# Gate logits of a cross-attention and mixture-of-experts block: gate weights held still in four column groups, tokens streamed

## The reference

```python
x = x + xattn(layernorm(x), ctx, ctx, mask, wq, bq, wk, bk, wv, bv, wo, bo)
xn2 = layernorm(x).reshape(8192, 512)
scores = softmax(xn2 @ w_gate)                 # [8192, 8]: the gate
weights, idx = top_k(scores, 2)
# each expert takes its tokens (at most 2048): h = xe @ c_fc; a, g = split(h)
# y = (silu(a) * g) @ c_proj; the sum of both, times their weights, is added to x
```

## Time and profile before

| | |
|---|---|
| median of 3 runs | 3031.32 us (3030.25 to 3031.86) |
| profiled execution | 3035.1 us, its span 3033.3 us |
| mean granted TensorE clock | 0.984 |
| busy, share of the span | TensorE 97%, weight loads 82%, VectorE 51%, ACT 51%, POOL 42% |

### The profile page before, as it was taken

How to read it: one execution, slowest core, us unless ns; L and a number is a source line. 1 busy time by engine, 2 the same in 40 slices (tenths; PEclk the granted TensorE clock), 3 DMA queues, 4 the chain that set the end, 5 groups by cost and what they waited for, 6 DMA issues and landing times.

```text
span 3033.3 us, 55379 instructions
## 1 busy us (share of the span) xinstructions
PE 2938.5 (97%) x17824; PEld 2489.2 (82%) x17824; DVE 1533.9 (51%) x5034; ACT 1542.7 (51%) x3910; POOL 1262.6 (42%) x1911
## 2 busy tenths in 40 slices
PE   6999999999999999994999999999999999999998
PEld 6888888888888888883788888888888888888886
DVE  5777777777777777773433223333242332423331
ACT  4777777777777777772323223233232322322321
POOL 4566666666666666664112122222212121222211
PEclk8999999999999999996999999999999999999999
DMA  5444444444444444432534343344434443444322
GB/s 162 124 126 132 124 122 127 126 132 124 124 126 125 133 125 124 125 104 83 135 87 101 77 98 78 90 88 91 86 94 88 94 94 77 98 80 94 68 44 28
DMA packets 290390, 315.35 MB, mean 104 GB/s; under 512 B 46528, under 2 KB 234944, under 8 KB 288576
## 3 DMA queue, kind: packets, MB, share of 16 engines
q1 hardware_dynamic: 227040, 178.48, 22.5%
q0 software_dynamic: 32768, 67.26, 12.8%
q10 hardware_dynamic: 30304, 66.07, 6.7%
HBM read 109.53 MB, written 67.90 MB: 58 GB/s over the span
## 4 chain that ended last, share of the span: by engine, by line
PE 51%; DMA 1%; SPq 0%; issue 0%; POOL 0%; DVE 0%; ACT 0%; POOLq 0%
PE a_ps L1219 17%; PE g_ps L1219 17%; PE y_ps L1234 17%; DMA out<-y,recs 0%; SPq L1012 0%; DMA xg<-xn_rows,gather_ids 0%; POOL xg L1058 0%; DMA lists<-table 0%; DMA x_quarters<-xg 0%; DVE xe_lo L1153 0%; POOL out L1086 0%; ACT xe_hi L1113 0%; DVE x_turned L1166 0%; ACT y L1146 0%; DVE act_part L1166 0%
## 5 line engine op out<-in xcount | busy, mean ns | idle before, releaser
L1086 POOL DMA_INDIRECT out<-y,recs x128 | 207.2, 1618 | 1185.7 <-ACT y L1146 751.8
L373 POOL TENSOR_SCALAR probs<-probs,row_inv 128x256 f32<-128x256 f32 x1024 | 492.3, 493 | 417.0 <-DVE row_inv L586 412.6
L577 DVE CUSTOM_DVE_ANT_0 probs<-scores_ps,mask_add,row_any 128x256 f32<-128x256 f32 x1024 | 454.6, 480 | 272.2 <-PE scores_ps L793 269.3
L1193 DVE TENSOR_TENSOR hidden<-act_part,g_ps 128x512 f32<-128x512 f32 x192 | 132.1, 688 | 860.0 <-ACT act_part L1132 860.0
L477 ACT ACTIVATE probs<-probs,low 128x256 f32<-128x256 f32 x1024 | 513.7, 504 | 99.9 <-DVE low L577 85.9
L462 ACT COPY probs_t<-probs_t_ps 128x512 f32<-128x512 f32 x512 | 299.9, 586 | 193.9 <-PE probs_t_ps L805 145.0
L1219 PE MATMUL a_ps<-xe_hi,fc_hi 128*128 128x512 f32 x768 | 300.3, 391 | 39.7 <-DVE xe_lo L1153 39.4
L805 PE MATMUL probs_t_ps<-ident,probs 128*128 128x128 f32 x2048 | 310.8, 274 | 7.5 <-POOL probs L373 7.5
L1219 PE MATMUL a_ps<-xe_lo,fc_hi 128*128 128x512 f32 x768 | 299.6, 390 | 0.0
L1219 PE MATMUL a_ps<-xe_hi,fc_lo 128*128 128x512 f32 x768 | 299.5, 390 | 0.0
L1219 PE MATMUL g_ps<-xe_lo,fc_hi 128*128 128x512 f32 x768 | 298.8, 389 | 0.0
(11 more groups left out here) (170 smaller groups left out, 6656.1 us busy)
## 6 DMA issues: line engine op xcount, KB each, us to landing
k_stack<-qk_hi SPq DMA_DIRECT2D x512, 64.0 KB, 2.0
q_stack<-qk_hi SPq DMA_DIRECT2D x512, 64.0 KB, 2.8
x_quarters<-xg SPq DMA_DIRECT2D x512, 64.0 KB, 2.0
fc_raw<-in_c_fc SPq DMA_DIRECT2D x24, 1024.0 KB, 5.8
k_stack<-qk_lo SPq DMA_DIRECT2D x256, 64.0 KB, 2.0
q_stack<-qk_lo SPq DMA_DIRECT2D x256, 64.0 KB, 2.9
out<-x_xn ACTq DMA_DIRECT2D x32, 512.0 KB, 3.3
xn_rows<-x_xn ACTq DMA_DIRECT2D x32, 512.0 KB, 3.6
```

The lines of the kernel that those rows point to most:

```text
L373: last = nc.gpsimd.tensor_scalar(probs[:, r, t, :], probs[:, r, t, :], row_inv[:, r, t:t + 1], 1.0, ALU.mult, ALU.mult)
L577: last = nc.vector.tensor_tensor_reduce(out=probs[:, s % 4, t, :], in0=scores_ps[s % 2][:, t, :], in1=mask_add[:, t, :], scale=row_any[:, ...
L1086: nc.gpsimd.indirect_dma_start(out=out[:, :], out_offset=bass.IndirectOffsetOnAxis(ap=recs[:, i * CT + t, 0:1].bitcast(U32), axis=0), in_= ...
L1193: nc.vector.tensor_tensor(hidden[:, m % 2, :], act_part[:, m % 2, :], g_ps[m % 2][:, :], ALU.mult).then_inc(gated, 1)
```

## The change

The gate weights are put into groups of 32 columns (`wg` is [128, 4, 32], cleared first, with the eight real columns loaded into each group). For each chunk c one matmul takes `wg[:, c, :]` as the stationary operand and all 256 tokens of the chunk as the moving one, and writes the partitions 32c to 32c+31 of `bank_b`: four partial products, transposed (experts in partitions), side by side. ACT copies them to `gate_parts` in SBUF. Two more matmuls, one for each tile of tokens, take `gate_parts` as the stationary operand and the constant `sum_parts` (a one where the partition is 32c + e for expert e) as the moving one; they add up the four parts and give the logits in the layout of before.

In the slots: the two transposes are at slots 10 and 11 and both go into `bank_a`, at slot 11 ahead of the matmuls of L820, so the second waits for the copy of the first. The gate matmuls are at slot 12 and wait for both copies; ACT's copy of the parts is at slot 12, the summing matmuls at slot 13. On POOL one more clearing stands first in the block, and a clearing with four selections behind its other constants. SP's load of wg waits for the clearing.

```diff
--- before.py
+++ after.py
@@ -98,7 +98,9 @@
         w_hi = sb("w_hi", [P, 4, DC, D], F32R)
         w_lo = sb("w_lo", [P, 4, DC, D], F32R)
         w_parts = (w_hi, w_lo)
-        wg = sb("wg", [P, DC, EXPERTS])
+
+        wg = sb("wg", [P, DC, DK])
+        sum_parts = sb("sum_parts", [P, EXPERTS])
         bias_qk = sb("bias_qk", [P, 2, DC])
         bias_v = sb("bias_v", [P, DC])
         bias_o = sb("bias_o", [P, D])
@@ -146,6 +148,7 @@
         shifted = sb("shifted", [P, 2, TILES])
         rstd = sb("rstd", [P, 2, TILES])
 
+        gate_parts = sb("gate_parts", [P, SEQ])
         logits = sb("logits", [P, TILES, EXPERTS])
         top = sb("top", [P, TILES, 8])
         top_at = sb("top_at", [P, TILES, 8], U32)
@@ -220,6 +223,10 @@
         xn2_stored = sem("xn2_stored")
         x2t_full = sem("x2t_full")
         x2t_ready = sem("x2t_ready")
+        wg_cleared = sem("wg_cleared")
+        sum_parts_ready = sem("sum_parts_ready")
+        gate_full = sem("gate_full")
+        gate_copied = sem("gate_copied")
         logits_full = sem("logits_full")
         logits_copied = sem("logits_copied")
         route_step = sem("route_step")
@@ -288,7 +295,8 @@
                         load_x(sp, 0, 0)
                         load_c(sp, 0)
                         load_w(0)
-                        sp.dma_start(wg[:, :, :], w_gate).then_inc(setup_loaded, 16)
+                        sp.wait_ge(wg_cleared, 1)
+                        sp.dma_start(wg[:, :, 0:EXPERTS], w_gate).then_inc(setup_loaded, 16)
                         sp.dma_start(bias_qk[:, :, :], b_qk).then_inc(setup_loaded, 16)
                         sp.dma_start(bias_v[:, :], b_v).then_inc(setup_loaded, 16)
                         sp.dma_start(bias_o[:, :], b_o).then_inc(setup_loaded, 16)
@@ -316,6 +324,7 @@
 
             @block.gpsimd
             def _(pool):
+                nc.gpsimd.memset(wg[:, :, :], 0.0).then_inc(wg_cleared, 1)
                 nc.gpsimd.memset(ident[:, :], 0.0).then_inc(pool_const, 1)
                 nc.gpsimd.memset(before[:, :], 0.0).then_inc(pool_const, 1)
                 nc.gpsimd.memset(zeros, 0.0).then_inc(pool_const, 1)
@@ -337,6 +346,13 @@
                                channel_multiplier=0, allow_small_or_imprecise_dtypes=True).then_inc(pool_const, 1)
                 nc.gpsimd.iota(tok_ids[:, :], pattern=[[P, TILES]], base=0, channel_multiplier=1,
                                allow_small_or_imprecise_dtypes=True).then_inc(pool_const, 1)
+
+                nc.gpsimd.memset(sum_parts[:, :], 0.0).then_inc(sum_parts_ready, 1)
+                for c in range(DC):
+                    pool.wait_ge(sum_parts_ready, c + 1)
+                    nc.gpsimd.affine_select(out=sum_parts[:, :], in_=sum_parts[:, :], compare_op=ALU.not_equal,
+                                            fill=1.0, base=-c * DK, pattern=[[-1, EXPERTS]],
+                                            channel_multiplier=1).then_inc(sum_parts_ready, 1)
 
                 def records(count, i):
 
@@ -463,13 +479,17 @@
                         if s == 14 and tail:
                             act.wait_ge(fall_ready, n)
                             nc.scalar.activation(weight_exp[:, :, :], fall[:, :, :], ACT.Exp).then_inc(weight_exped, 1)
-                        if s in (10, 12) and tail:
-                            t = (s - 10) // 2
+                        if s in (10, 11) and tail:
+                            t = s - 10
 
                             act.wait_ge(x2_stored, n * 16)
                             act.wait_ge(x2t_full, n * TILES - TILES + t + 1)
-                            nc.scalar.copy(x2t[:, :, t * P:(t + 1) * P], (bank_a, bank_b)[t][:, :].rearrange(
+                            nc.scalar.copy(x2t[:, :, t * P:(t + 1) * P], bank_a[:, :].rearrange(
                                 "p (c i) -> p c i", c=DC)).then_inc(x2t_ready, 1)
+                        if s == 12 and tail:
+                            act.wait_ge(gate_full, n)
+                            need(act, logits_full, n - 1)
+                            nc.scalar.copy(gate_parts[:, :], bank_b[:, 0:SEQ]).then_inc(gate_copied, 1)
                         if heads:
 
                             act.wait_ge(masked, g + 1)
@@ -806,6 +826,16 @@
                                                                probs[:, h % 4, t, u * P:(u + 1) * P],
                                                                ident[:, :])
                             last.then_inc(turned, 1)
+                        if s in (10, 11) and tail:
+                            t = s - 10
+                            pe.wait_ge(xn2_ready, n)
+                            if t:
+                                pe.wait_ge(x2t_ready, (n - 1) * TILES + 1)
+                            elif proj:
+                                pe.wait_ge(k_ready, (n + 1) * DC + DC)
+                            else:
+                                pe.wait_ge(v_ready, BATCH * TILES)
+                            transposed(bank_a, xn2, t, x2t_full)
                         if (s - LAG) % HPC == 0 and (tail if s <= LAG else heads):
                             c = ((s - LAG) // HPC - 1) % DC
                             par, of = (p, n) if s > LAG else (q, n - 1)
@@ -833,29 +863,28 @@
                             else:
                                 need(pe, q_ready, n * DC + 2)
                             transposed((bank_a, bank_b)[t], xn, t, xt_full)
-                        if s in (10, 12) and tail:
-                            t = (s - 10) // 2
-                            pe.wait_ge(xn2_ready, n)
-                            if not proj:
-                                pe.wait_ge(v_ready, BATCH * TILES)
-                            elif t:
+                        if s == 12 and tail:
+                            if is_step(n, 1):
+
+                                pe.wait_ge(setup_loaded, 80)
+                                pe.wait_ge(dve_const, 6)
+                            if proj:
                                 pe.wait_ge(q_ready, (n + 1) * DC + 2)
                             else:
-                                pe.wait_ge(k_ready, (n + 1) * DC + DC)
-                            if not heads:
                                 pe.wait_ge(x2_ready, (n - 1) * TILES + 1)
-                            transposed((bank_a, bank_b)[t], xn2, t, x2t_full)
+                            pe.wait_ge(x2t_ready, n * TILES)
+                            for c in range(DC):
+                                last = nc.tensor.matmul(bank_b[c * DK:(c + 1) * DK, 0:SEQ], wg[:, c, :],
+                                                        x2t[:, c, :], start=True, stop=True)
+                            last.then_inc(gate_full, 1)
                         if s == 13 and tail:
                             if is_step(n, 1):
-
-                                pe.wait_ge(setup_loaded, 80)
-                                pe.wait_ge(dve_const, 6)
-                            pe.wait_ge(x2t_ready, n * TILES)
+                                pe.wait_ge(sum_parts_ready, DC + 1)
+                            pe.wait_ge(gate_copied, n)
                             for t in range(TILES):
-                                for c in range(DC):
-                                    last = nc.tensor.matmul(bank_b[:, t * EXPERTS:(t + 1) * EXPERTS],
-                                                            x2t[:, c, t * P:(t + 1) * P], wg[:, c, :],
-                                                            start=(c == 0), stop=(c == DC - 1))
+                                last = nc.tensor.matmul(bank_b[:, t * EXPERTS:(t + 1) * EXPERTS],
+                                                        gate_parts[:, t * P:(t + 1) * P], sum_parts[:, :],
+                                                        start=True, stop=True)
                             last.then_inc(logits_full, 1)
                         if s == 15 and tail:
 
@@ -912,7 +941,7 @@
                                     pe.wait_ge(w_split, 3)
                                 pe.wait_ge(k_ready, (n + 1) * DC + DC)
                                 if tail:
-                                    pe.wait_ge(x2t_ready, (n - 1) * TILES + 1)
+                                    pe.wait_ge(x2t_ready, n * TILES)
                             if s == 14:
                                 pe.wait_ge(q_ready, (n + 1) * DC + DC)
                             rows((bank_a, bank_c)[t], 2, [part[:, q] for part in ct], t, v_full,
```

More of the change, by code:

```diff
@@ L835, in step @@
                             transposed((bank_a, bank_b)[t], xn, t, xt_full)
-                        if s in (10, 12) and tail:
-                            t = (s - 10) // 2
-                            pe.wait_ge(xn2_ready, n)
-                            if not proj:
-                                pe.wait_ge(v_ready, BATCH * TILES)
-                            elif t:
-                                pe.wait_ge(q_ready, (n + 1) * DC + 2)
```

(26 more changed lines are left out.)

## The result

The change made the kernel faster by half a per cent: 3015.49 us, the median of five runs (3013.93 to 3017.34), beside 3030.65 us for the kernel before (five runs, 3028.62 to 3031.86), a ratio of 0.9951 with the 95% interval 0.9936 to 0.9965. That is 15.2 us; the forecast was 14.9. Run again later on another chip, the changed kernel took 3013.88 us (3012.95 to 3016.2) beside 3030.63, a ratio of 0.9945 (0.9932 to 0.9959), which is 16.7 us. The profiled execution took 3016.34 us, with a span of 3014.5.

What follows compares the result with a forecast made beforehand. TensorE was taken to bound the batch steps: 30 steps at 0.58 us less give -17.4, plus 1.8 stall, 0.5 last steps and 0.2 wg load, -14.9 us; from the median 3031.32 that is 3016.4 us, range 3011 to 3026.

Steps and rivals of the forecast that it cites:

- The bound: Batch steps, 200 to 700 us: TensorE never idles, so work taken from its stream saves time one for one.
- What goes: Slot 13: the 16 records of the old logits matmuls, bound by the loading of weights, leave; 1.78 us a step saved.
- the sum: Slot 13: two f32 summing matmuls, 4 records of the old logits' kind, add 0.45 us a step.
- The gate: Slot 12: four gate matmuls in two rounds of 0.22 us, with entry and exit, add 0.75 us; bounds 0.68 to 0.9.
- The moved transposes: Second set of xn2 transposes, slot 12 to slot 11: costs the same in either place, zero, bounds 0.1 either way.
- The stall at slot 14: Projection at slot 14 waits for qk_lo, tied to the load of x: 0.06 us a step, 1.8 us in all.
- Rival (a): VectorE's chain decides: late qk_hi or x stalls each step about 0.3 us at slot 14; 3023 us; chance 0.17.
- Rival (b): Slot 12: gate matmuls don't run side by side, eight rounds for two; 3053 us; chance 0.06 with its half-way form.
- Rival (c): No change: another engine fills the step as TensorE does; 3029 to 3031 us; chance 0.09.
- The last steps: Last step, nothing overlapping: the new path to the logits takes 0.2 us more; with step 31, 0.5 us together.
- The two small terms: Added outside the steps: 0.5 us for the last steps, 0.2 us at the start for the DMA into wg.

Runs made afterwards that it cites:

- The second gates: The changed kernel with the four gate matmuls run once more: directly behind the first, at slot 14, or at slot 15; 3027.11, 3037.82 and 3028.88 us.

## Why the prediction was right

- **The bound** held: TensorE is busy 500 of 500 us, and less work in its stream was less time, one for one, until the cover was gone.
- **What goes**, 1.78 us, and **the sum**, 0.45: slot 13 fell by 1.32, forecast 1.33. That the 8 moving columns don't set the price fits the transposes, whose records with 128 moving columns also start 0.11 us apart; that the loading of weights does, no run tests by itself.
- **The gate**, 0.75: slot 12 rose by 0.35; with 0.43 for the transposes that left, it is 0.78 (0.74 in the step shown), inside 0.68 to 0.9. The second gates show the parts as they were taken: two rounds of 0.22 and 0.3 for the way in and out.
- **The moved transposes**, 0: 42.074 beside 42.094, and 0.41 for 0.43.
- **The stall at slot 14**, 0.06: 0.03 by the slot's length. The reasoning behind it, a chain tied to the load of x that doesn't come earlier when TensorE does, was confirmed by taking the gate out (slot 14 longer by 1.15 us) and by moving the load (the step shorter by 0.61). The prediction gave the semaphore 0.1 to 0.2 us; the wait that can be read took 0.06. Rival (a) had the right chain and the wrong size: it begins to decide 0.26 us further on, the cover that is left.
- **Rival (b)**, gate matmuls one after the other, was refuted by the trace and then built: with one column group the kernel takes 3063.64. The reading weighed there of the Trainium skill (TensorE: Matmul & The Clock Gate, Part 3, matmuls in strict order) as five rounds for two doesn't hold: the 8 records of four matmuls run in two rounds, 0.24 us apart. Which two records belong to one matmul the trace doesn't say, so it doesn't test the order itself.
- **Rival (c)**: no other engine took the time back.
- **The last steps**: from the first transposes to VectorE's copy it is 6.47 us in place of 6.32, 0.15 more, forecast 0.2 (0.15 by its own figures). The rows of the last step, at a granted clock of 0.50 as before, answer to the earlier trace rows:

```profile
1380.81 1.12 PE L768 MATMUL bank_a<-ident,x_xn 128*128 128x128 f32 x4 [4.76 <-DVE x_xn L565]
...
1384.66 1.08 PE L877 MATMUL bank_b<-x_xn,wg 128*32 128x256 f32 x8 [0.82 <-ACT x_xn L487]
...
1386.22 1.02 PE L885 MATMUL bank_b<-sum_parts,gate_parts 128*128 128x8 f32 x4 [0.48 <-ACT gate_parts L492]
1387.28 0.17 DVE L671 COPY logits<-bank_b 128x16 f32<-128x16 f32 x1 [6.52 <-PE bank_b L885]
```

Two things in the sum were off and nearly cancelled. The step got shorter by 0.587 us, forecast 0.52 with the stall: 30 x 0.07 = 2 us that the forecast lacks, all in the slots that the change doesn't touch. And the 17.6 us of the steps became 15.2 in the medians. Only one execution of each kernel is profiled, so where the other 2.4 went can't be read from them; in the parts outside the 30 steps single executions differ by as much. From the start of the span to slot 0 of step 1 they take 82 to 85.2 us, and from slot 0 of step 31 to the first expert matmul 98.1 to 101.7 (107.3 in the kernel without the gate and with x earlier).

The two small terms for these parts can't be confirmed for the same reason. For the last steps together the forecast adds 0.5 us, but from slot 0 of step 31 it is 100.29 us before and 98.91 after (99.27 with only the moves, 98.13 in the repeat). For the start it adds 0.2 us for the scattered load of wg, a guess: the load lands 6.3 us after its issue in both kernels, and step 1 begins at 85.20 and 85.12 us.

So the mechanism was right, and part of the closeness is luck: the first pair of medians is 15.2 us apart, the second 16.7, and the forecast of 14.9 is nearer to the first than its working deserves.

## What to carry to other kernels

Count a small matmul by its rounds, not by its columns: 16 records with a new stationary each for 8 moving columns cost 1.78 us, and the same product with the weights stationary, in four column groups side by side, 0.75 plus 0.45 for the sum. Put work of a tiled form next to other work of that form; each excursion among untiled matmuls cost 0.3 us, and moving the gate next to its own form took another 0.24 us off the step, beside the 0.59 of the change itself. Before taking more from the bound engine, measure the cover of the next chain and where its root lies: 0.26 us was left here. And look at what stands behind a load in its queue before moving it: issued a slot earlier in ACT's queue, the load of x held up a copy by 0.9 us and the stacks behind it by 0.6, and that kernel was 7 to 9 us slower, while the same move in the kernel with the gate at slot 11 cost nothing that could be told.

## What was not expected of the hardware

- From the start of slot 0 to the start of slot 9 the step is shorter in every kernel made from the changed one, with the same instructions in it (medians 22.19 to 22.25, beside 22.279 before and 22.279 with only the moves). 0.08 us a step are 2.4 us in all. The changed kernels differ from the other two there in where their tensors lie in SBUF, as wg is larger and two tensors are new; whether that is the cause no run tests.
- Two summing matmuls with 32 rows cost 0.27 us more than with 128.
- The kernel without the gate has no shorter steps than the one with it (means 41.588 and 41.507): once the chain decides, TensorE's own work is free.
